# Full-array products gathered in two of the four macros of an attention pair

## The reference

```
lat = layer_norm(layernorm(x)); ctx = layer_norm(ctx_1024)
q = lat @ Wq;  k, v = split(ctx @ Wkv);  k = apply_rope(k, cos, sin)
attn = softmax(clip(q k^T / 8, -11, 11))
x = x + (attn @ v) @ Wo + bo
sel = sigmoid(xn . expert_sel); h = relu(xn @ keys[e]);  x = x + sum_e sel_e * (h_e @ values[e])
```

## Time and profile before

| | us |
|---|---|
| median of 3 runs | 1029.39 |
| profiled execution, its own time | 1029.17 |
| its span, first to last instruction | 1027.4 |
| TensorE busy | 980.8 (95%) |
| VectorE busy | 824.6 (80%) |
| ScalarE busy | 508.6 (50%) |
| GpSimd busy | 252.6 (25%) |
| attention pairs, about | 35.6 to 829 |
| feed-forward phase, about | 829.8 to 1027.4 |

### The profile page before, as it was taken

One profiled execution on the slowest core, in us unless ns is written; L12 is line 12 of the kernel. 1 busy time (PEld: TensorE's weight loads), 2 busy tenths in 40 slices (PEclk: granted clock), 3 DMA queues, 4 the chain that ended last, 5 costly groups with the idle time before them and its releaser, 6 DMA issues. The chain is left out here.

```text
span 1027.4 us, 15252 instructions
## 1 busy us (share of the span) xinstructions
PE 980.8 (95%) x5336; PEld 603.2 (59%) x5336; DVE 824.6 (80%) x1226; ACT 508.6 (50%) x735; POOL 252.6 (25%) x228
## 2 busy tenths in 40 slices
PE   3989999999999999999999999999999789999998
PEld 2745555555555555555555555555555358888886
DVE  7799999989899989999988888998889976545422
ACT  4655455555656555555555655555555542222221
POOL 3454323111112111111112000321000145445443
PEclk9999999999999999999999999999999999999999
DMA  5543323332323223222333222232222471242221
GB/s 157 186 144 95 109 84 93 99 96 78 106 86 90 88 73 89 73 88 73 97 81 91 64 83 83 83 83 83 84 64 76 131 253 56 114 128 116 106 83 42
DMA packets 68952, 100.34 MB, mean 98 GB/s; under 512 B 21968, under 2 KB 44752, under 8 KB 66832
## 3 DMA queue, kind: packets, MB, share of 16 engines
q1 hardware_dynamic: 68880, 99.41, 32.0%
HBM read 70.01 MB, written 10.75 MB: 79 GB/s over the span
## 5 line engine op out<-in xcount | busy, mean ns | idle before, releaser
L1102 ACT ACTIVATE wide_a<-score_ps 128x1024 f32<-128x1024 f32 x256 | 249.1, 1030 | 148.2 <-PE score_ps L904 148.2
L1366 DVE TENSOR_SCALAR wide_a<-wide_a 128x1024 f32<-128x1024 f32 x256 | 183.9, 749 | 73.9 <-ACT wide_a L1102 73.8
L1375 DVE TENSOR_TENSOR p_sum<-wide_a 128x1024 f32<-128x1024 f32 x128 | 162.6, 1270 | 2.3
L917 PE MATMUL o_ps<-wide_a,values_a 128*64 128x512 f32 x512 | 124.0, 605 | 1.5 <-DVE wide_a L1366 1.5
L917 PE MATMUL o_ps<-wide_a,v_sb 128*64 128x512 f32 x512 | 124.0, 605 | 0.0
L904 PE MATMUL score_ps<-q_hi,k_hi 64*128 64x512 f32 x512 | 114.7, 445 | 2.6 <-DVE k_lo L1345 1.9
L1908 DVE SCALAR_TENSOR_TENSOR act<-h_ps,wide_a 128x512 f32<-128x512 f32 x64 | 44.2, 690 | 90.0 <-PE h_ps L149 83.2
L904 PEld LDWEIGHTS score_ps<-q_hi,k_hi 64*128 64x128 f32 x512 | 48.0, 184 | 112.2 <-issue 97.8
L1679 POOL TENSOR_TENSOR act_lo<-act,act_hi 128x512 fp32r<-128x512 f32 x64 | 84.8, 1325 | 96.5 <-ACT act_hi L1825 96.5
L1825 ACT CAST act_hi<-act 128x512 fp32r<-128x512 f32 x64 | 39.7, 621 | 135.7 <-DVE act L1908 135.7
L904 PE MATMUL score_ps<-q_hi,k_lo 64*128 64x512 f32 x512 | 101.4, 392 | 0.0
(11 more groups left out here) (232 smaller groups left out, 2013.8 us busy)
## 6 DMA issues: line engine op xcount, KB each, us to landing
wide_a<-sel_dram SPq DMA_DIRECT2D x16, 1024.0 KB, 4.7
k_swap<-k SPq DMA_DIRECT2D x124, 128.0 KB, 2.3
w_hi<-packs_hi SPq DMA_DIRECT2D x26, 384.0 KB, 3.9
w_lo<-packs_lo SPq DMA_DIRECT2D x26, 384.0 KB, 4.6
den<-inv_dram SPq DMA_DIRECT2D x64, 128.0 KB, 2.9
ctx_raw<-ctx SPq DMA_DIRECT2D x24, 128.0 KB, 2.3
packs_hi<-w_hi SPq DMA_DIRECT2D x8, 384.0 KB, 3.4
packs_lo<-w_lo SPq DMA_DIRECT2D x8, 384.0 KB, 3.7
```

The costliest lines, as they stand in the source:

```text
L917: mm = pe.matmul(o_ps[DH * h:DH * h + DH, :], v_sb[n // 2 % 2][:, at:at + DH], probs[s % RING][:, h, :], start=(s == 0), stop=(s == STEPS ...
L1102: act.activation(probs[s % RING][:], score_ps[s % 2][:], ACT.Exp, scale=DH ** -0.5).then_inc(exp_done, 1)
L1366: dve.tensor_scalar(probs[s % RING][:], probs[s % RING][:], CLIP_HI, CLIP_LO, ALU.min, ALU.max).then_inc(clipped, 1)
L1375: dve.tensor_tensor(p_sum[m][:], first, second, ALU.add).then_inc(summed_up, 1)
```

## The change

On TensorE, y1 of pair n-3 now comes in macro 0 of pair n, ahead of K (it was in macro 2 of pair n-1). The query product, both V halves and y0 come in macro 2, in the order query, V half 0, y0, V half 1, and then the transposes. Macros 1 and 3 have no full-array product left, but for pair 0 (the last duo of the prologue is transposed in macro 1) and pair 31 (y1 of pair 29 in macro 3). ScalarE's roundings and copies follow the products into macro 2. On VectorE the tile is normalized ahead of clip 2, the two rope products stand between clips 2 and 3, `split_q` comes after macro 1's `sum_up` and ahead of `invert_den`, and `rope_add` after that; `scale_o` and the first `sum_quad` move from macro 3 to macro 2, `add_y` of y0 to macro 2 and of y1 to macro 0 of the next pair.

```diff
--- before.py
+++ after.py
@@ -981,17 +981,26 @@
                 for m in range(MACROS):
                     scores(n, 2 * m)
                     scores(n, 2 * m + 1)
+                    if m == 0 and n >= 3:
+                        pe.wait_ge(y_added, 2 * (n - 3) + 1)
+                        project_y(pe, sh, n - 3, 1, side_ps, w_hi[n % 2], w_lo[n % 2], (n - 1) % 2)
                     if m == 0 and p < NPAIR:
                         project_k(p, 0)
                         project_k(p, 1)
                     if n == 0 and m == 1:
                         pe.wait_ge(v_stored, FILLS)
                         turn_first(FIRST_DUOS - 1)
-                    if m == 1 and p < NPAIR:
+                    if m == 2 and p < NPAIR:
                         pe.wait_ge(k_evac, 2 * p + 1)
                         q_product(p)
-                    if m == 1 and n + 2 < NPAIR:
+                    if m == 2 and n + 2 < NPAIR:
                         project_v(n, 0)
+                    if m == 2 and n >= 2:
+                        pe.wait_ge(den_evac, n)
+                        pack_ready(n - 2 + WO_LAG)
+                        project_y(pe, sh, n - 2, 0, side_ps, w_hi[p % 2], w_lo[p % 2], n % 2)
+                    if m == 2 and n + 2 < NPAIR:
+                        project_v(n, 1)
                     if m == 2 and t < TILES:
                         pe.wait_ge(normed, blocks(t + 1))
                         pe.wait_ge(v_stored, FILLS + 2 * n + 1)
@@ -1006,15 +1015,9 @@
                             pe.wait_ge(head_split, 2)
                             pe.wait_ge(sel_split, 1)
                             logits(pe, sh, job_ps[1], lambda k: xT_hi[:, 0, k, :], lambda k: xT_lo[:, 0, k, :])
-                    if m == 3 and n + 2 < NPAIR:
-                        project_v(n, 1)
-                    if n >= 2 and m in (1, 2):
-                        if m == 1:
-                            pe.wait_ge(den_evac, n)
-                            pack_ready(n - 2 + WO_LAG)
-                        else:
-                            pe.wait_ge(y_added, 2 * (n - 2) + 1)
-                        project_y(pe, sh, n - 2, m - 1, side_ps, w_hi[p % 2], w_lo[p % 2], n % 2)
+                    if m == 3 and n == NPAIR - 1:
+                        pe.wait_ge(y_added, 2 * (n - 2) + 1)
+                        project_y(pe, sh, n - 2, 1, side_ps, w_hi[p % 2], w_lo[p % 2], n % 2)
                     if m > 0:
                         attend(n, 2 * m - 2)
                         attend(n, 2 * m - 1)
@@ -1174,14 +1177,15 @@
                             evac_k(p, 1)
                         if n > 0:
                             evac_o(n - 1)
-                    if m == 1:
+                    if m == 2:
                         if p < NPAIR:
                             round_q(p)
                         if n + 2 < NPAIR:
                             store_v(j, FILLS + 2 * n)
-                    if m == 2:
                         if p < NPAIR:
                             round_k(p)
+                        if n + 2 < NPAIR:
+                            store_v(j, FILLS + 2 * n + 1)
                         if t < TILES:
                             act.wait_ge(turned, t - FIRST_TILES + 1)
                             wait(act, tile_split, blocks(t))
@@ -1191,8 +1195,6 @@
                         if n == 28:
                             exp_gate(act, sh, 0, job_ps[1])
                     if m == 3:
-                        if n + 2 < NPAIR:
-                            store_v(j, FILLS + 2 * n + 1)
                         if n in (24, 26):
                             round_keys((n - 24) // 2)
                     if n == NPAIR - 1 and m in (1, 2):
@@ -1450,21 +1452,25 @@
             def iteration(n):
                 p, t = n + 1, n + FIRST_TILES
                 for m in range(MACROS):
-                    if m == 2 and p < NPAIR:
-                        rope_add(p)
-                    if m == 3 and n >= 2:
+                    last = n == NPAIR - 1
+                    if m == 1 and t < TILES:
+                        wait(dve, turned, t - FIRST_TILES)
+                        normalize(t, ctx_n[:], x_n[:])
+                    if last and m == 3:
                         add_y(dve, sh, n - 2, 1, side_ps, bo)
-                    last = n == NPAIR - 1
-                    if last and m == 3:
                         split_keys(3)
                     clip(n, 2 * m)
                     if last and m == 3:
                         scale_o(dve, sh, n - 1)
+                    if m == 1 and p < NPAIR:
+                        rope_times(p)
                     clip(n, 2 * m + 1)
-                    if m == 1 and p < NPAIR:
-                        split_q(p)
                     if m == 0 and n > 0:
                         sum_quad(n - 1, 1)
+                    if m == 0 and n >= 3:
+                        add_y(dve, sh, n - 3, 1, side_ps, bo)
+                    if m == 2 and n >= 2:
+                        add_y(dve, sh, n - 2, 0, side_ps, bo)
                     sum_up(n, m)
                     if m == 0:
                         if t < TILES:
@@ -1474,27 +1480,24 @@
                         if n == 29:
                             invert_gate(dve, sh, 0, 0)
                     if m == 1:
-                        if t < TILES:
-                            wait(dve, turned, t - FIRST_TILES)
-                            normalize(t, ctx_n[:], x_n[:])
+                        if p < NPAIR:
+                            split_q(p)
                         if n > 0:
                             invert_den(dve, sh, n - 1)
-                        if n >= 2:
-                            add_y(dve, sh, n - 2, 0, side_ps, bo)
                         if p < NPAIR:
-                            rope_times(p)
+                            rope_add(p)
                     if m == 2:
                         if last:
                             sum_quad(n, 0)
                         if p < NPAIR:
                             split_k(p)
-                        if n == 29:
-                            invert_gate(dve, sh, 0, 1)
-                    if m == 3:
                         if n > 0 and not last:
                             scale_o(dve, sh, n - 1)
                         if not last:
                             sum_quad(n, 0)
+                        if n == 29:
+                            invert_gate(dve, sh, 0, 1)
+                    if m == 3:
                         if n == 23:
                             split_sel()
                         if n in (24, 25):
```

## The result

The changed kernel takes 1025.97 us (median of 20 runs, 1023.93 to 1030.71), the kernel before 1029.51 beside it (20 runs, 1028.36 to 1030.8): a ratio of 0.9967, 95% interval 0.996 to 0.9973. So it is 3.5 us faster, not 12.4, and its time lies 2 us outside the range. In one of the experiments, e3, one run of six took 1211.9 us at a mean granted clock of 0.756; the median given for e3 counts it, the ratio does not.

What follows compares the result with a forecast made beforehand. VectorE and TensorE were taken to bound it side by side (24.45 and 24.31 us a pair); -1.0 + 3.5 + 7.5 + 4.0 - 0.2 - 1.3 = 12.5 us off 1029.17, said as 1017.0, range 1012.5 to 1024.

Steps and rivals of the forecast that it cites:

- the second of the new waits: V half 1 in macro 2 waits for the query remainder; 2.1 us of products were to cover 1.3 us.
- VectorE's: 6 x 0.6: Pairs 1 to 6, taken as bound by VectorE: 0.6 us saved in each, 3.5 us together.
- up to 6 us for this: Pairs 1 to 5: the sum falls by this much if GpSimd blocks both rope products by 1.3 us.
- the sum for the new waits: Five new waits over all pairs: 1.3 us subtracted, bounds 0 and 0.5 a pair, 15 us.
- loop (1): attend(n, 0) behind macro 1's scores needs o_raw copied; today's lag would cost 0.6 us, expected to shrink to zero.
- attend(n, 0) waiting for o_evac: Sign that the forecast is wrong: TensorE waits at attend(n, 0) for the copy of o_raw; no size given.
- Small waits in some pairs: Inverse of the denominators ahead of scale_o: 5.2 us of cover against 4.9 at the median, 0.3 us left.
- Term (5): SyncE's fetch of the weights waits for y1 in the next pair's macro 0: no cost but in pair 30.
- C: The end: last inverse waits behind 2.8 MB, 3 to 4 us; pair 0 loses 3; 1022 us, chance 0.12.
- A: VectorE stays the bound because the inverse lands late, 0.6 us a pair: 1024 us, chance 0.15.
- B: TensorE's handovers between matmul forms stay, only VectorE's part gains: 1024.5 us, chance 0.05.
- D: Slower: the inverse's wait at scale_o delays all of macro 3, over 0.75 us a pair: 1035 us, chance 0.08.

Runs made afterwards that it cites:

- e3: Changed kernel with VectorE's order of the kernel before, save for the y additions and the rope addition: median 1110.94 us, ratio 1.0786 to the kernel before.
- e13: Changed kernel with pair 0's query remainder moved right behind clip 2: median 1024.47 us, ratio 0.9947 to the kernel before.
- e5: Changed kernel with pair 0 in its old order and V half 1 back in macro 3 in every pair: 1027.49 us, ratio 0.9975 to the kernel before.
- e6: Changed kernel with pair 0 in its old order and V half 1 in macro 3 in pairs 0 to 6 only: 1021.06 us, ratio 0.992.
- e1: Changed kernel with pair 0 alone put back to its old order on TensorE, ScalarE and VectorE: 1023.68 us, ratio 0.9945 to the kernel before.
- e9: e1 with GpSimd's remainder of the projection weights cut to 8 of 768 columns: 1014.63 us, ratio 0.9861 to the kernel before.
- e10: Kernel before the change with GpSimd's remainder of the weights cut to 8 of 768 columns: 1023.47 us, ratio 0.9941.
- e4: VectorE's new order alone on TensorE's and ScalarE's order of the kernel before: 1031.94 us, ratio 1.0023 to the kernel before.
- e8: e1 with the denominators' inversion put ahead of the query remainder: 1021.94 us, ratio 0.9926 to the kernel before.
- e12: Changed kernel with pairs 0 to 6 in the old order on all engines, inversion ahead of the remainder from pair 7: 1020.54 us, ratio 0.991.
- e7: e1 with the query remainder ahead of macro 1's sum in pairs 1 to 5: 1021.57 us, ratio 0.9918 to the kernel before.
- e11: Changed kernel with pairs 0 to 6 in the old order on all engines, later pairs as changed: 1021.82 us, ratio 0.992.

## Why the prediction was wrong

**Pair 0, the largest miss (-5.1 against -1.0).** The failed step is the second of the new waits: "V half 0 and y0 (2.1 us) cover the rounding and the subtraction (1.3) ahead of V half 1." That weighed the two operations of the chain and left out what stands in front of the subtraction on VectorE: in pair 0 two rope products, clip 3 and the sum, 7.1 us from 48.3 to 55.4, with no y0 to cover (TensorE had done V half 0 by 48.7), and the first rope product stretched to 2.82 us beside GpSimd. The step looked at VectorE's wait for the root instead, which cost almost nothing by itself: in e13 it stays and the denominators come at 67.93. In four of the pairs 1 to 5 the same wait appears with 0.8 to 2.4 us; there it hid no gain, as e5 and e6 show.

**Pairs 1 to 6 (-0.3 against +3.5).** "VectorE's: 6 x 0.6" counted idle time and took the busy time as fixed. The idle time did go: 152.08 - 138.93 = 13.2 us before, 152.37 - 142.15 = 10.2 now. But busy time rose by 3.2. VectorE's clips in this stretch, before and after (count, then busy us, mean ns, and idle time before them):

```profile
L1366 DVE TENSOR_SCALAR wide_a<-wide_a 128x1024 f32<-128x1024 f32 x48 | 38.3, 835 | 11.8 <-ACT wide_a L1102 11.8
```
```profile
L1368 DVE TENSOR_SCALAR wide_a<-wide_a 128x1024 f32<-128x1024 f32 x48 | 43.1, 926 | 3.3 <-ACT wide_a L1105 3.2
```

The idle time in front of the clips fell by 8.5 us; 4.8 of it went into longer clips, 4.2 into the wait for the root that now stands in the same place (16.2 us over all pairs). In the old order VectorE stood idle (94.5 to 96.6 us in the pair of the earlier trace rows) while GpSimd took the root and rounded the weights, and the split met two clips; in the new order clip 2, a rope product and clip 3 stand beside it, in the pair at 97 us of e1 with 2.02, 1.63 and 1.78 us. e9 and e10 show a part of the price as caused by the split, 2.8 us; that the rest of the longer busy time comes of GpSimd's other work is argued from such rows, not shown. With pair 0 in its old order (e1) the stretch loses 1.4 us where 3.5 were forecast, a miss of 4.9: 2.8 are this contention, and the other 2.1 would not have come without it either, since TensorE then bounds at 24.29 us a pair (145.76 / 6) against 24.53 in the old order, 1.4 us in six pairs. (In the changed kernel itself 1.1 us less is lost, behind the stall of pair 0; why is not shown.)

The Trainium skill, SBUF — State Buffer, SBUF: two separate sides, says that VectorE and GpSimd lock one shared port pair for a whole instruction, and that a VectorE operation with two SBUF inputs contends with a GpSimd operation that reads SBUF. The trace agrees: in pair 0 GpSimd's split ran from 47.71 to 50.04 us, and the rope product that started beside it at 48.30 ended 1.1 us behind it, after 2.82 us instead of 1.2. The prediction named up to 6 us for this and gave it no chance of its own, though it was the likelier price.

**Pairs 7 to 20 (+4.0 against +7.5).** The mechanism held: TensorE is busy 336.1 of 338.4 us, VectorE idles ahead of normalizing and clip 2, and but for three waits for the inverse nowhere else. The size of TensorE's gain was nearly right. e4 measures 24.40 and 24.23 us for the old order, 24.31 as computed; the new one takes 24.05 in even pairs and 23.86 in an odd pair in which nothing waits (pair 7 of e6). Two sections so bring 0.35 and 0.37, not 0.39, and 0.40 in pairs 22 and 23, which have no tile transposes (23.60 and 23.65 us against 24.01 before). That is 0.5 us of the 3.5 missing.

The step that failed is the sum for the new waits, 1.3 us over all pairs: they took 3.0 in this stretch alone. The first is loop (1), of which the prediction said that "the lag shrinks to zero, and the wait with it": in the seven odd pairs, which have fewer transposes, TensorE waits at attend(n, 0) for the copy of o_raw, and the pair takes some 24.05 again (24.00 to 24.08 where nothing else waits): 7 x 0.19 = 1.3 us. This is the sign "attend(n, 0) waiting for o_evac" that the prediction had listed itself. The second is the inverse: 338.38 - 14 x 24.05 = 1.7 us of irregular waits, in the profile on scale_o and behind it on attend(n, 0). "Small waits in some pairs" named it; e8 takes 1.4 us of it back.

**Pairs 21 to 29 (+2.7 against +4.0)**: the same, and two waits for the remainder (1.4 and 0.5 us at 645 and 670 us). The first stands behind 2.59 us in which VectorE waits for k_swap. Term (5), the order on SyncE, was put at nothing but in pair 30; here its loads of weights and of keys, issued from 630.0 us, stand right ahead of K's swap at 633.4, where before they stood 12 us ahead of it and VectorE did not wait. That these loads delayed the swap is argued, not shown. **The end (+0.6 against -0.2)**: inside its bounds; TensorE waits 2.8 us there for y1's addition where it waited 3.62 for a sum, VectorE 0.3 for den_rows (the sign of C), so C's end came in kind but cost nothing.

**The rivals.** A was half right: the inverse comes late, but irregularly, 4.8 us over the whole and not 0.6 a pair. B fell: the direct handover takes 0.32 to 0.35 us where nothing waits, and no product stands in macros 1 and 3 of the middle pairs. C named pair 0 with 3 us and the wrong cause. D fell; VectorE's wait for the inverse is 4.8 us in 29 pairs, far from 0.75 a pair (one was 1.5). None had the loop of TensorE and VectorE through the query remainder, nor contention that grows when idle time is filled. The signs to look for were good where named: normalizing inside the idle time came true, VectorE waiting for exponentials 0 and 1 did not, and for q_hi it waited in four pairs only: at 24.05 us the two engines are in step, neither is ahead.

## What to carry to other kernels

When a remainder or copy is moved behind other work on its engine, count the whole queue ahead of it in the worst iteration, the prologue's, not the length of the operation: here 7 us of queue in one pair took 5.1 us, 3.9 of it for good by pair 7. Idle time on VectorE beside GpSimd's work is not free to fill; see first what GpSimd runs in it. And where an order helps only the steady state, switch to it where that begins: e12 keeps the old start and takes the whole gain of the middle.

## What the runs showed of the hardware

TensorE's clock fell to 1.2 GHz in pair 0 of the changed kernel within 7.4 us of idling (granted 0.94 from 48 to 52 us, 0.50 from 52 to 60, 0.78 from 60 to 64). After waits of 2.4 us it fell in part in two profiles (0.61 from 104 to 108 us in e1, 0.69 from 108 to 112 in the changed kernel) and not in a third: e13 has the same wait of 2.42 us at 106 us, and the granted clock stays at 1.00. In e5 and e6, without these waits, it was 1.00 over pairs 1 to 6. Where it fell, waiting cost more than the wait: in pair 0 V half 1 and attend took 2.2 us longer.

The store of the inverse, 4 KB, has a median of 1.4 us from issue to landing, but now and then the spread behind it starts 3.4 us later. SyncE in the changed kernel, ahead of its longest wait for the inverse, and VectorE behind it:

```profile
523.96 0.33 SPq L185 DMA_DIRECT2D inv_dram<-inv_rows  x1
527.36 1.10 SPq L192 DMA_DIRECT2D den<-inv_dram  x2
```
```profile
530.79 0.69 DVE L200 TENSOR_TENSOR o_raw<-o_raw,den 128x512 f32<-128x512 f32 x1 [1.50 <-DMA den<-inv_dram]
```

The late store is not mere chance: pair 20, with this wait, takes 25.06 or 25.07 us in the profiles of the changed kernel, e1, e7 and e11, and 24.07 or 24.08 in those of e6, e8, e12 and e13. What delays it stays open, and no run delayed these transfers on purpose. Whether such waits spread the changed kernel's runs (1023.9 to 1028.4 us and one at 1030.7) isn't shown either: e11 spreads over 2.9 us, e12, where the inverse is issued 0.6 us earlier, over 2.3, with five runs each; and the slowest run of the changed kernel is also the one with the lowest mean clock, 0.988.
